# An attention and feed-forward layer: weights streamed in quarters through two half buffers, masks loaded one at a time

## What is computed

```python
def _layernorm(x, axis=-1, eps=1e-5):
    m = jnp.mean(x, axis=axis, keepdims=True)
    v = jnp.var(x, axis=axis, keepdims=True)
    return (x - m) / jnp.sqrt(v + eps)

def attn(x, Wq, bq, Wk, bk, Wv, bv, Wo, bo):       # 16 heads of 64
    # summary: mean of x over windows of 64 positions that end at 0, 64, 128, ... (128 of them)
    summary = (end_sum - prev_sum) / lengths
    q = x @ Wq + bq                                # every token
    k, v = summary @ Wk + bk, summary @ Wv + bv    # 128 rows
    scores = einsum('bhtd,bhcd->bhtc', q, k) / 8
    scores = where(ends <= position, scores, -inf)
    return einsum('bhtc,bhcd->bhtd', softmax(scores), v) @ Wo + bo

def ffn(x, w_fc, b_fc, w_proj, b_proj):            # hidden width 4096
    # block_quant: blocks of 32 share an exponent, mantissas of 3 bits
    h = gelu(block_quant(x) @ block_quant(w_fc).T + b_fc)
    return block_quant(h) @ block_quant(w_proj).T + b_proj

x = x + attn(_layernorm(x), ...)
x = x + ffn(_layernorm(x), ...)
```

## Time and profile before

| | us |
|---|---|
| median of three runs | 2365.01 (2364.59 to 2365.13) |
| the profiled execution | 2365.58 |
| its span, slowest core | 2363.4 |
| spans of the 8 cores | 2354.1 to 2363.4 |
| stage 1, from the windows of the trace | 0 to 648 |
| stage 2 | 648 to 704 |
| stage 3, four rounds | 704 to 870, 1034, 1198 and 1365 |
| stage 4 | 1365 to 2363 |
| busy: PE, DVE, ACT, POOL | 1026.5, 986.4, 525.3, 149.8 |

### The profile page before, as it was taken

How to read it: one execution, slowest core, us unless ns; L and a number is a source line. 1 busy time by engine, 2 the same in 40 slices (tenths; PEclk the granted TensorE clock), 3 DMA queues, 4 the chain that set the end, 5 groups by cost and what they waited for, 6 DMA issues and landing times.

```text
span 2363.4 us, 17452 instructions; the slowest of 8 cores (2354.1 to 2363.4 us)
## 1 busy us (share of the span) xinstructions
PE 1026.5 (43%) x5088; PEld 462.5 (20%) x5088; DVE 986.4 (42%) x1750; ACT 525.3 (22%) x934; POOL 149.8 (6%) x268
## 2 busy tenths in 40 slices
PE   1212221212223334423514456666666666666667
PEld 0101010111111211211202122222222222222222
DVE  5666667666501310311112134444444444444443
ACT  1111111111201402212212122222222222222222
POOL 1111110101000200201102000000000000000000
PEclk9999999999965566556656677778888777777778
DMA  3333333333143133133132110000000000000000
GB/s 81 73 79 80 78 74 89 89 82 92 40 86 74 36 106 54 31 94 71 18 107 54 36 36 18 18 19 18 18 18 18 18 19 18 18 12 15 11 18 18
DMA packets 69356, 114.42 MB, mean 48 GB/s; under 512 B 36480, under 2 KB 36496, under 8 KB 67216
## 3 DMA queue, kind: packets, MB, share of 16 engines
q0 software_dynamic: 19392, 37.77, 9.8%
q1 hardware_dynamic: 49872, 75.55, 9.7%
HBM read 134.29 MB, written 16.78 MB: 64 GB/s over the span
## 4 chain that ended last, share of the span: by engine, by line
DVE 30%; PE 29%; issue 15%; ACT 14%; DMA 9%; POOL 2%; DVEq 1%; ACTq 0%; SPq 0%; POOLq 0%
PE psC L998 10%; PE psE L238 4%; DVE wstr L390 3%; DVE qa_amax L973 3%; DMA wbuf<-wq_in 3%; ACT hqT L246 2%; DVE bnscr L464 2%; DVE hbuf L217 2%; DVE hqb L220 2%; DVE bnscr L466 2%; DMA xmid_scr<-xmid_t 1%; POOL ebuf L770 1%; DMA wbuf<-wo_in 1%; DMA xring<-xown 1%; ACT wfcTq L246 1%
## 5 line engine op out<-in xcount | busy, mean ns | idle before, releaser
L998 PE MATMUL psC<-wpjTq,hqT 128*128 128x512 bf16 x1024 | 295.8, 451 | 64.6 <-ACT hqT L246 64.6
L238 PE MATMUL psE<-ident,wqnat 128*128 128x128 bf16 x256 | 37.4, 300 | 424.2 <-DVE qa_e L343 397.0
L773 DVE TENSOR_REDUCE ssum<-ebuf 128x16 f32<-128x2048 bf16 x16 | 36.5, 2283 | 294.8 <-POOL ebuf L770 294.8
L998 PEld LDWEIGHTS psC<-wpjTq,hqT 128*128 128x128 bf16 x1024 | 108.7, 112 | 229.8 <-issue 163.4
L973 DVE TENSOR_REDUCE qa_amax<-hbuf 128x64 f32<-128x2048 f32 x32 | 73.2, 2286 | 138.5 <-ACT hbuf L963 135.7
L238 PEld LDWEIGHTS psE<-ident,wqnat 128*128 128x128 bf16 x256 | 22.2, 126 | 446.6 <-issue 446.6
L238 PE MATMUL psE<-ident,hqb 128*128 128x128 bf16 x256 | 30.5, 256 | 174.7 <-DVE hqb L220 174.7
L246 ACT ACTIVATE hqT<-psE 128x512 bf16<-128x512 f32 x64 | 38.2, 597 | 286.1 <-PE psE L238 286.1
L217 DVE TENSOR_TENSOR hbuf<-hbuf,qa_eb 128x1024 f32<-128x1024 f32 x64 | 78.4, 1225 | 50.0 <-PE psD L238 44.4
L942 PE MATMUL psA<-wfcTq,xqfm 128*128 128x512 bf16 x256 | 98.6, 385 | 0.9 <-ACT xqfm L246 0.9
L946 PE MATMUL psA<-wfcTq,xqfm 128*128 128x512 bf16 x256 | 98.3, 384 | 0.0
(11 more groups left out here) (232 smaller groups left out, 1963.0 us busy)
## 6 DMA issues: line engine op xcount, KB each, us to landing
xsq<-xseq POOLq DMA_DIRECT2D x32, 512.0 KB, 6.5
wstr<-wfc_in SPq DMA_DIRECT2D x32, 512.0 KB, 3.6
wstr<-wpj_in SPq DMA_DIRECT2D x16, 1024.0 KB, 6.0
xring<-xown SPq DMA_DIRECT2D x16, 512.0 KB, 6.3
mexp<-mask_in SPq DMA_DIRECT2D x16, 512.0 KB, 6.3
wbuf<-wq_in POOLq DMA_DIRECT2D x8, 1024.0 KB, 8.1
wbuf<-wo_in POOLq DMA_DIRECT2D x8, 1024.0 KB, 8.1
xmid_scr<-xmid_t SPq DMA_DIRECT2D x16, 512.0 KB, 2.7
```

The lines of the kernel that those rows point to most:

```text
L238: E.matmul(d, s, ident[:, :], start=True, stop=True),
L998: S.op("tensor", lambda E, c_=c, cc=cl, cjj=cj, s_=gs: E.matmul(psC[:, cc:cc + 512], hqT[:, 1024 * s_ + 128 * cjj:1024 * s_ + 128 * cjj + ...
```

## The change

- A helper, `wstream`, takes over the weight loads of K, V, Q and the output projection. wbuf is used as two half buffers of two blocks each, with a semaphore of its own for each (WBF, WBF2). A matrix comes in four quarters of 512 KB. Quarters 0 and 1 are issued together, behind all matmuls so far; quarter q + 2 behind the matmuls of quarter q, into the same half buffer.
- The matmul loops run over a quarter's two blocks. Their number and shapes are the same.
- The early load of Wo's first half at the end of `p1_lnq` is gone; all four quarters are loaded in `p1_wo_res`.
- mexp has one slot. `mask_expand(t + 1)` puts the next mask's load on SP right behind the multiply of tile t; `mask_expand(0)` stands ahead of the first loads of x.
- lnbuf has two slots, by the parity of the tile, and ACT's wait is for the transposes of the tile two before.

```diff
+        def wstream(wview, quarter_fn, nq=4):
+            marks = {}
+            sems = {}
+
+            def issue(q):
+                buf3 = wbuf.ap().rearrange("p (h k f) -> p h k f", h=2, f=D)[:, q % 2, :, :]
+                sem = "WBF" if q % 2 == 0 else "WBF2"
+                S.wait_at("gpsimd", "PE", marks.get(q - 2, S.c("PE")))
+                S.op("gpsimd", lambda E, b=buf3, q_=q: E.dma_start(
+                    out=b, in_=wview[:, 2 * q_:2 * q_ + 2, :]), inc=sem, amt=16)
+                return sem, S.c(sem)
+
+            sems[0] = issue(0)
+            if nq > 1:
+                sems[1] = issue(1)
+            for q in range(nq):
+                S.wait_at("tensor", sems[q][0], sems[q][1])
+                buf = wbuf[:, (q % 2) * 2 * D:(q % 2) * 2 * D + 2 * D]
+                quarter_fn(q, buf)
+                marks[q] = S.c("PE")
+                if q + 2 < nq:
+                    sems[q + 2] = issue(q + 2)
...
-        for hf in range(2):
-            S.wait_at("gpsimd", "PE", S.c("PE"))
-            S.op("gpsimd", lambda E, h=hf: E.dma_start(
-                out=wbuf.ap().rearrange("p (k f) -> p k f", f=D),
-                in_=wk_v[:, 4 * h:4 * h + 4, :]), inc="WBF", amt=16)
-            S.wait_at("tensor", "WBF", S.c("WBF"))
+
+        def k_quarter(q, buf):
             for m in range(8):
-                for kl in range(4):
-                    k = 4 * hf + kl
-                    S.op("tensor", lambda E, m_=m, k_=k, kk=kl: E.matmul(
+                for kl in range(2):
+                    k = 2 * q + kl
+                    S.op("tensor", lambda E, m_=m, k_=k, kk=kl, b=buf: E.matmul(
                         kdst[m_],
-                        wbuf[:, kk * D + m_ * 128: kk * D + m_ * 128 + 128],
+                        b[:, kk * D + m_ * 128: kk * D + m_ * 128 + 128],
                         summ_fm[:, k_ * 128:k_ * 128 + 128],
                         start=(k_ == 0), stop=(k_ == 7)),
-                        inc="PE" if (m == 7 and kl == 3) else None)
+                        inc="PE" if (m == 7 and kl == 1) else None)
+        wstream(wk_v, k_quarter)
...
-        lnbuf = sb1("lnbuf", [128, D], BF16)
+        lnbuf = sb1("lnbuf", [128, 2 * D], BF16)
...
-        mexp = sb1("mexp", [128, 2 * 16 * 128], BF16)
+        mexp = sb1("mexp", [128, 16 * 128], BF16)
...
+        lnq_pe = {}
+
+        def mask_expand(tt):
+            S.wait_at("sync", "GE", S.c("GE"))
+            dma("sync", "MSK0",
+                mexp.ap().rearrange("p (g c) -> p g c", c=128),
+                mask_in.rearrange("(t p) c -> p t c", p=128)[:, tt, :]
+                .unsqueeze(1).broadcast_to([128, 16, 128]))
+            msk_marks[tt] = S.c("MSK0")
...
+        mask_expand(0)
...
+                lsl = (t % 2) * D
+                S.wait_at("scalar", "PE", lnq_pe.get(t - 2, 0))
...
+                lnq_pe[t] = S.c("PE")
...
+            wstream(wq_v, q_quarter)
...
-            S.wait_at("gpsimd", "PE", S.c("PE"))
-            wo_v = wo_in.rearrange("(k p) f -> p k f", p=128)
-            S.op("gpsimd", lambda E: E.dma_start(
-                out=wbuf.ap().rearrange("p (k f) -> p k f", f=D),
-                in_=wo_v[:, 0:4, :]), inc="WBF", amt=16)
...
-            S.wait_at("sync", "GE", S.c("GE"))
-            msem = "MSK0" if u % 2 == 0 else "MSK1"
-            dma("sync", msem,
-                mexp.ap().rearrange("p (s_ g c) -> p s_ g c", s_=2, c=128)[:, u % 2, :, :],
-                mask_in.rearrange("(t p) c -> p t c", p=128)[:, t, :]
-                .unsqueeze(1).broadcast_to([128, 16, 128]))
-            msk_marks[t] = (msem, S.c(msem))
...
-            S.wait_at("gpsimd", msk_marks[t][0], msk_marks[t][1])
+            S.wait_at("gpsimd", "MSK0", msk_marks[t])
             S.op("gpsimd", lambda E, e=e3, mk=m3: E.tensor_tensor(
                 out=e, in0=e, in1=mk, op=ALU.mult), inc="GE")
+            if t + 1 < NT:
+                mask_expand(t + 1)
...
-                if hf == 1:
-                    S.wait_at("gpsimd", "PE", S.c("PE"))
-                    S.op("gpsimd", lambda E: E.dma_start(
-                        out=wbuf.ap().rearrange("p (k f) -> p k f", f=D),
-                        in_=wo_v[:, 4:8, :]), inc="WBF", amt=16)
-                S.wait_at("tensor", "WBF", S.c("WBF"))
...
+            def wo_quarter(q, buf):
...
+            wstream(wo_v, wo_quarter)
...
```

More of the change, by code:

```diff
@@ L589, in build_nc, with v_quarter @@
         wv_v = wv_in.rearrange("(k p) f -> p k f", p=128)
-        for hf in range(2):
-            S.wait_at("gpsimd", "PE", S.c("PE"))
-            S.op("gpsimd", lambda E, h=hf: E.dma_start(
-                out=wbuf.ap().rearrange("p (k f) -> p k f", f=D),
-                in_=wv_v[:, 4 * h:4 * h + 4, :]), inc="WBF", amt=16)
-            S.wait_at("tensor", "WBF", S.c("WBF"))
+        def v_quarter(q, buf):
             for cl in (0, 512):
                 vdst = psB[:, 0:512] if cl == 0 else psD[:, 0:512]
-                for kl in range(4):
-                    k = 4 * hf + kl
-                    S.op("tensor", lambda E, k_=k, kk=kl, c=cl, dd=vdst: E.matmul(
+                for kl in range(2):
+                    k = 2 * q + kl
+                    S.op("tensor", lambda E, k_=k, kk=kl, c=cl, dd=vdst, b=buf: E.matmul(
                         dd, summ_fm[:, k_ * 128:k_ * 128 + 128],
-                        wbuf[:, kk * D + c: kk * D + c + 512],
+                        b[:, kk * D + c: kk * D + c + 512],
                         start=(k_ == 0), stop=False),
-                        inc="PE" if (cl == 512 and kl == 3) else None)
-            if hf == 1:
+                        inc="PE" if (cl == 512 and kl == 1) else None)
+            if q == 3:
                 S.wait_at("tensor", "LG", S.c("LG"))
@@ L612, in build_nc @@
                     start=False, stop=True), inc="PE")
+        wstream(wv_v, v_quarter)
         w("scalar", "PE")
@@ L700, in p1_lnq, with q_quarter @@
             wq_v = wq_in.rearrange("(k p) f -> p k f", p=128)
-            for hf in range(2):
-                S.wait_at("gpsimd", "PE", S.c("PE"))
-                S.op("gpsimd", lambda E, h=hf: E.dma_start(
-                    out=wbuf.ap().rearrange("p (k f) -> p k f", f=D),
-                    in_=wq_v[:, 4 * h:4 * h + 4, :]), inc="WBF", amt=16)
-                S.wait_at("tensor", "WBF", S.c("WBF"))
+            def q_quarter(q, buf):
                 for m in range(8):
-                    for kl in range(4):
-                        k = 4 * hf + kl
-                        S.op("tensor", lambda E, m_=m, k_=k, kk=kl: E.matmul(
-                            qdst[m_], wbuf[:, kk * D + m_ * 128: kk * D + m_ * 128 + 128],
+                    for kl in range(2):
+                        k = 2 * q + kl
+                        S.op("tensor", lambda E, m_=m, k_=k, kk=kl, b=buf: E.matmul(
+                            qdst[m_], b[:, kk * D + m_ * 128: kk * D + m_ * 128 + 128],
                             ln1fm[:, k_ * 512:(k_ + 1) * 512],
                             start=(k_ == 0), stop=(k_ == 7)),
-                            inc="PE" if (m == 7 and kl == 3) else None)
+                            inc="PE" if (m == 7 and kl == 1) else None)
+            wstream(wq_v, q_quarter)
             w("scalar", "PE")
@@ L824, in p1_wo_res @@
                         dd = odst[u][half]
-                        for ml in range(4):
-                            m = 4 * hf + ml
-                            S.op("tensor", lambda E, m_=m, mm=ml, c=cl, u_=u, d=dd: E.matmul(
+                        for ml in range(2):
+                            m = 2 * q + ml
+                            S.op("tensor", lambda E, m_=m, mm=ml, c=cl, u_=u, d=dd, b=buf: E.matmul(
                                 d, ofm[:, m_ * 512 + 128 * u_: m_ * 512 + 128 * u_ + 128],
-                                wbuf[:, mm * D + c: mm * D + c + 512],
+                                b[:, mm * D + c: mm * D + c + 512],
                                 start=(m_ == 0), stop=False),
-                                inc="PE" if (u == 3 and half == 1 and ml == 3) else None)
-                        if hf == 1:
+                                inc="PE" if (u == 3 and half == 1 and ml == 1) else None)
+                        if q == 3:
                             S.wait_at("tensor", "LG", S.c("LG"))
```

18 lines of the change are left out of this document (5 added, 13 removed).

## The result

The changed kernel takes 2306.18 us in the median of 8 runs (2300.41 to 2311.01); the kernel before, run beside it, 2365.53 (2364.59 to 2368.04). The ratio is 0.9745, interval 0.9732 to 0.9759: 59 us less, where 57 was forecast. The profiled execution took 2309.3 us; its spans are 2293.5 to 2307.0 us, against a slowest core of 2363.4 before.

A forecast was written before the change was run, and what follows sets the result against it. No engine but a chain of handovers, crossing 16 open weight loads per core, was taken as the bound. Savings of 33 + 7 + 12 + 3 + 2 = 57 us from 2365.6 gave 2308 us, range 2288 to 2337.

The forecast's parts named there:

- Load length: Weight loads into wbuf: a 512 KB quarter lands in 6.0 us, range 5.6 to 6.5; the xsq cast load took 6.3.
- The DMA view's rate: One Q load in the trace: about 210 GB/s after 1.3 us of nothing, giving 5.6 us for a quarter.
- slow quarters: Rival on the weight loads: quarters take 6.7 to 7.5 us, costing 14 to 30 us of the gain; chance 0.09.
- a loss: Rival on the weight loads: two quarters in flight delay each other, sign turns at about 8.4 us, kernel slower; chance 0.06.
- Q, 33 forecast: Q projection, four times: 34.1 us from first issue becomes 25.8, 8.3 saved each time, 33 us in all.
- The clock: PE after the gap before a third quarter: falling to half clock costs 1.7 to 1.8 us; half, 0.9, was added.
- wo, 7 forecast: Output projection, four times: 31.3 us becomes 29.5, 1.8 saved each time, 7 us in all; called the weakest term.
- K and V, 12 forecast: K and V stage, once each: 6.6 us saved in K and 5.4 in V, 12 us in all.
- The masks in attention, 3 forecast: Attention rounds: second multiply waits for its mask, DVE's scaling is no longer slowed; 0.75 us a round, 3 in all.
- The masks and xown, gain of 2 forecast: Round starts: masks no longer behind xown loads, 1 us earlier in three rounds, 1 later in the first; net 2.
- lnbuf, 0: Layer norm: the second lnbuf slot gains 0, since ACT's preceding eviction had already waited for the same transposes.
- The late mask: Rival in attention: masks land in 6.3 us instead of 3.7, 2.4 us lost a round, 2318 us; chance 0.05.

The follow-up runs named there:

- e_wo_early: The changed kernel with quarters 0 and 1 of Wo issued right after the Q projection, at the end of `p1_lnq`; 2277.23 us.
- e_ln1: The changed kernel with one lnbuf slot and the old wait again; 2307.15 us.
- e_mask2: The changed kernel with two mask slots and the mask loads of before again, and one lnbuf slot; 2309.7 us.
- e_mask2_ve: e_mask2 plus one wait: a round's second mask multiply on POOL starts only when DVE has scaled the first tile; 2311.5 us.

## Why the prediction was right, step by step

The mechanism was right: loads beside matmuls shorten the chain. That the sum came within 2 us of the measured gain is in part luck: Q and the attention brought 7 us more than forecast, wo, K and V and the loads of x brought 8 less, and 3 us of the profiled difference lie in the untouched feed-forward. Steps of one projection in the kernel after, mean of 8 cores and 4 rounds, from the timelines of POOL, PE and ACT:

| us | Q forecast | Q | wo forecast | wo |
|---|---|---|---|---|
| first issue to first matmul | 6.14 | 5.63 | 6.14 | 5.70 |
| first quarter's matmuls | 5.1 | 5.44 | 6.3 | 5.73 |
| second quarter and the gap | 6.65 | 6.47 | 6.65 | 6.61 |
| third quarter | 4.35 | 4.31 | 4.35 | 5.04 |
| fourth, to the next engine | 3.55 | 3.71 | 6.45 | 7.09 |

- *Load length.* Forecast 6.0 (5.6 to 6.5); measured 5.6 and 5.4 in the median of all, 5.3 and 5.4 for the first quarter that PE stands for. The DMA view's rate gave 5.6 and was the better bracket; xsq pulled me up. The rivals of slow quarters and of a loss fell with it. By the fit of the Trainium skill ("DMA: Bandwidth & Descriptors", "Anatomy of one DMA") the prediction had worked out 6.9 us; the trace disagrees. The second of two joint quarters lands 7.1 us after its own issue and did not hold PE up in Q and wo.
- *Q, 33 forecast, 38.4 measured.* The forecast length was nearly exact (25.8 from first issue, measured 25.6). The base was off: I read one round, 34.1 us from issue, and it was the shortest of 32 (their mean is 1.1 longer).
- *The clock.* I charged half a fall, 0.9 us, after each gap. For Q that was right in the mean: 15 of 32 third quarters ran wholly at the full clock (3.45 to 3.48 us), most others in 4.9 to 5.2. For wo 29 of 32 took 4.75 us or more. The gap before it is alike in both (6.47 and 6.61 us from the second quarter's start), and e_wo_early has the same gap and 27 of 32 at the full clock; it differs in that PE comes to the stream from attention without the open load. One thing goes with it: how long after a stream's first matmul the clock rose to full, in the mean 4.7 us in wo, 4.2 in Q and 3.8 in e_wo_early's wo. Over the 320 streams of these two kernels, e_ln1, e_mask2 and e_mask2_ve, none of the 94 fell in the third quarter that had risen within 4.0 us and then idled at most 3.3, and all 135 did that rose after 4.5 us or later. No experiment moved the one without the other, so this is a regularity and not a shown cause.
- *wo, 7 forecast, 4.4 measured.* The fall above cost 0.7 a round. Eight bias matmuls stand among fewer others: two matmuls and a bias one take 0.86 us, so the last quarter took 0.6 longer than I had put. The shorter first quarter gave 0.6 back and the shorter load 0.4. The base was off here too: 31.3 us from the first matmul in the printed chain, 31.0 in the mean of 8 cores and 4 rounds.
- *K and V, 12 forecast, 10.2 measured.* Again the base: the chain's core had the longest stage of the eight (55.8, mean 52.8). The lengths after were close: 21.6 and 21.8 us forecast for K and V, 21.0 and 21.8 in the mean. The 8.98 and 8.24 us of the chain are second quarters, issued 0.7 us behind the first.
- *The masks in attention, 3 forecast, 4.6 measured.* The new wait came as forecast (4.2 us behind the first multiply) and cost nothing, since DVE's scaling is no longer slowed. That the two slow each other is shown by e_mask2_ve. The Trainium skill ("SBUF — State Buffer", "Who interferes with whom") says that a DVE instruction with two inputs in SBUF contends with a GpSimd instruction that reads SBUF, that the shared ports are an exclusive lock, and that the order of issue decides who blocks. The rows fit: before, DVE started 1.2 us ahead of the multiply's end and took 1.0 longer; after, POOL started 0.95 us ahead of the scaling's end and took 0.8 longer.
- *The masks and xown, gain of 2 forecast, loss of 1.7 measured.* This term had the wrong sign. I took the slow mask loads to delay xown in every round; the three later rounds gained 0.3 each and the first lost 2.6. There the mask delays SP's own issues as well, which I had priced at 0.4 each.
- *lnbuf, 0:* right (e_ln1).

The late mask did not come about: the median landing is 3.8 us.

```profile
DMA to landing us min/median/max: 3.4/3.8/6.3
```

## What to carry to other kernels

Where a chain of waits crosses whole loads, cut them into pieces and keep two or more in flight; pieces alone are a loss (57 us in K, V and Q here). A third slot of the same size brought 33 us, eighths in four slots of the same memory 43. Ask of each load whether it can be issued before the engine stands, also across the end of its matrix: having no load of Wo ahead of the attention cost 29 us beside a gain of 59, and loads that run ahead pay part of their gain back to the stores beside them. Take the base of a saving from all cores and rounds, not from the one chain that is printed.

## What was not expected

- The same code came out of a gap in PE's work of about 2.6 us at either clock, so one Q projection took 23.6 to 27.9 us on different cores and rounds.
- Four load issues on SP took 4.12 us behind a mask's load and 1.95 without it (one core each; from the first issue to the fourth 2.7 against 1.3 in the mean of 8).
- A store of 2.6 us took 6.57 beside a weight load that POOL had issued 0.9 us earlier, although the store is on SP's queue.
- Loads issued together land one behind the other, each counted from its own issue (medians for Q): three quarters after 5.5, 7.4 and 9.1 us, four eighths after 3.9, 4.7, 5.7 and 6.4.
